# Routing tokens two chunks at a time, and moving steps of a fused attention and mixture-of-experts kernel

## What is computed

```python
x = x + tanh(g_xattn) * (softmax(q @ concat(ctx, k_new).T / 16) @ concat(ctx, v_new)) @ wo.T   # of layernorm(x)
...
probs = softmax(xf @ gate_w.T); top_p, top_i = top_k(probs, 2)
y = sum over the two experts of top_p * (silu(xf @ fc1.T) * (xf @ fc2.T)) @ proj.T
y = y + sigmoid(xf @ shared_gate_w.T) * (silu(xf @ s_fc1.T) * (xf @ s_fc2.T)) @ shared_proj.T
x = x + tanh(g_ffn) * y
```

## Time and profile before

| | |
|---|---|
| median of 3 runs (lowest, highest) | 294.89 us (294.42, 295.42) |
| the profiled execution's own time | 294.28 us |
| its span | 292.5 us |
| busy: PE, DVE, ACT, POOL | 93%, 73%, 58%, 47% of the span |
| granted clock of TensorE, mean | 0.999 |
| chain that ended last, by engine | PE 57%, DVE 23%, issue 7%, ACT 6%, DMA 3% |
| stages, by start | opening 0, chunk 0 about 17, chunk 1 about 41, chunk 2 about 65, chunk 3 about 88, shared blocks about 110, experts about 180, tail about 267 |

### The profile page before, as it was taken

The page is one execution under the profiler, slowest core; times in us unless marked ns, Lnnn a source line. Parts: engine busy times, 40 slices in busy tenths (PEclk is TensorE's granted clock), DMA queues, the critical chain, the costliest instruction groups (busy, mean ns, idle before and its releaser), DMA issues.

```text
span 292.5 us, 5859 instructions
## 1 busy us (share of the span) xinstructions
PE 272.9 (93%) x1777; PEld 245.7 (84%) x1777; DVE 213.9 (73%) x694; ACT 170.7 (58%) x401; POOL 136.1 (47%) x161
## 2 busy tenths in 40 slices
PE   3998899999899899999999999899999999999992
PEld 3887789789778677888788888899999999998882
DVE  6867776979869759768776767868778777763285
ACT  2775678687566567473335446566666667654240
POOL 2420831441784427453450000068778778776141
PEclk9999999999999999999999999999999999999999
DMA  6470244221136112544425744368888888756796
GB/s 194 190 256 2 73 149 141 72 80 50 38 91 242 74 40 85 186 144 125 150 76 182 247 140 145 131 113 134 136 141 134 136 139 137 116 69 72 291 354 217
DMA packets 25022, 40.18 MB, mean 137 GB/s; under 512 B 2976, under 2 KB 18976, under 8 KB 24992
## 3 DMA queue, kind: packets, MB, share of 16 engines
q1 hardware_dynamic: 16272, 27.43, 29.1%
q0 software_dynamic: 7152, 9.57, 19.4%
q10 hardware_dynamic: 1568, 2.80, 2.7%
HBM read 22.68 MB, written 17.11 MB: 136 GB/s over the span
## 4 chain that ended last, share of the span: by engine, by line
PE 57%; DVE 23%; issue 7%; ACT 6%; DMA 3%; POOL 1%; SPq 0%; DVEq 0%; ACTq 0%; POOLq 0%
PE bank L437 43%; PE bank L702 8%; DVE ew_lo L1097 4%; DMA xn_all<-x_dram 3%; PE bank L801 3%; PE bank L755 3%; DVE work L1453 2%; ACT ew_hi L830 2%; DVE xt_lo L1097 2%; ACT sh_hi L830 2%; DVE neg_max L1145 2%; DVE sh_lo L1097 2%; DVE ln_stats L1108 1%; DVE work L1168 1%; ACT work L862 1%
## 5 line engine op out<-in xcount | busy, mean ns | idle before, releaser
L1650 POOL DMA_INDIRECT y_d<-work,dest_of_slot x39 | 60.5, 1552 | 56.2 <-DVE dest_of_slot L1504 54.7
L437 PE MATMUL bank<-ew_hi,xt_hi 128*128 (+2 forms) x172 | 53.9, 323 | 1.4 <-DVE xt_lo L1097 0.7
L437 PE MATMUL bank<-ew_lo,xt_hi 128*128 (+2 forms) x172 | 51.7, 301 | 0.0
L437 PE MATMUL bank<-ew_hi,xt_lo 128*128 (+1 forms) x133 | 40.5, 305 | 0.0
L1610 POOL DMA_INDIRECT xs_d<-xn_all,slot_of_pair x32 | 33.3, 1042 | 10.1 <-issue 7.3
L1097 DVE TENSOR_TENSOR xt_lo<-bank,xt_hi 128x256 fp32r<-128x256 f32 (+2 forms) x90 | 35.5, 397 | 3.2 <-ACT xt_hi L830 2.0
L437 PE MATMUL bank<-xt_hi,sw_hi 128*128 128x512 f32 x88 | 34.8, 395 | 0.2 <-DVE work L1453 0.2
L437 PE MATMUL bank<-xt_lo,sw_hi 128*128 128x512 f32 x88 | 34.5, 392 | 0.0
L437 PE MATMUL bank<-xt_hi,sw_lo 128*128 128x512 f32 x88 | 34.3, 390 | 0.0
L830 ACT ACTIVATE xt_hi<-bank 128x256 fp32r<-128x256 f32 (+1 forms) x90 | 32.7, 409 | 2.4 <-PE bank L801 1.1
L437 PEld LDWEIGHTS bank<-ew_hi,xt_hi 128*128 128x128 f32 (+1 forms) x172 | 32.4, 189 | 2.0 <-DVE xt_lo L1097 0.9
(11 more groups left out here) (161 smaller groups left out, 678.8 us busy)
## 6 DMA issues: line engine op xcount, KB each, us to landing
work<-xs_d SPq DMA_DIRECT2D x39, 136.0 KB, 2.5
weight_stage<-ew_dram SPq DMA_DIRECT2D x10, 486.5 KB, 3.7
y_d<-work SPq DMA_DIRECT2D x6, 512.0 KB, 3.9
work<-ctx_t_dram SPq DMA_DIRECT2D x4, 512.0 KB, 3.3
ew_hi<-y_d SPq DMA_DIRECT2D x4, 512.0 KB, 8.1
ew_hi<-y_d ACTq DMA_DIRECT2D x4, 512.0 KB, 7.0
xn_all<-x_dram SPq DMA_DIRECT2D x3, 512.0 KB, 6.6
xs_d<-pad_row SPq DMA_DIRECT2D x9, 136.0 KB, 2.0
```

The lines of the kernel that those rows point to most:

```text
L437: last = nc.tensor.matmul(dst, a, b, start=(n == 0), stop=(n == len(pairs) - 1))
L1650: nc.gpsimd.indirect_dma_start(out=y2_d, out_offset=bass.IndirectOffsetOnAxis(ap=IX[:, n:n + 1], axis=0), in_=EY[:, n % 4, :], in_offset=None,
```

## The change

What it does, part by part:

1. **Opening.** SP loads x of chunk 1 before the context of chunk 0. ACT loads the constants before the gates. TensorE's empty products (`warm`) are 13, 0, 3 in place of 10, 4, 4. DVE does `project_lo(0, 0)` after the lo parts of the weights, `ln1_stats(2)` after `row_max(0, 2)`, and `project_lo(1, 0)` before `residual(0, 0)`.
2. **Chunks 1 and 2.** In chunk 1 `scores` alternate with `first_norm`. In chunk 2 `attend(2, 2)` and `residual(2, 2)` come after the last projection.
3. **Routing.** Two passes of 8 tiles in place of four of 4. The first (chunks 0, 1): `shifted`, `route_exp` in chunk 2, all else in chunk 3, with `slots(0)` after `aggregate(3, 0)`; `attend` doesn't wait for it. The second (chunks 2, 3) in the shared blocks, at the places of the old fourth one. POOL scatters chunk 0 in chunk 3 and the others after it.
4. **Tail.** `fc` 2 and 3, and 4 and 5, stand together; the multiply of block 5 comes before `s_lo(4)`; POOL's `combine(6)` waits for the last `s_lo`; DVE's `combine(7)` comes before `s_last`.

```diff
+GT = 2 * TPC
+N_GR = N_T // GT
...
+            load_x(1)
             sp.dma_start(CR, ctx_t[0]).then_inc(d_ct, 16)
-            load_x(1)
...
-                if j == 1 and c > 1:
-                    waits = waits + [(0, v_pos, c - 1)]
...
-            def route(c):
-                bank, o = (B[1], 0) if c == LAST else (B[7], D)
+            def route(g):
+                bank = B[4] if g == 0 else B[1]
...
-            warm(10)
+            warm(13)
             first_norm(0, 0)
-            warm(4)
             first_norm(0, 1)
-            warm(4)
+            warm(3)
...
-                if 0 < c < LAST:
+                if c == 1:
                     first_norm(c + 1, 0)
+                    scores(c, 0)
                     first_norm(c + 1, 1)
-                scores(c, 0)
-                scores(c, 1)
+                    scores(c, 1)
...
-                if c > 1:
-                    route(c - 2)
...
                 attend(c, 1)
+                if c == LAST:
+                    route(0)
...
-                attend(c, 2)
+                if c != LAST - 1:
+                    attend(c, 2)
                 values(c, 3)
                 probs_t(c, 3)
                 if c < LAST:
                     project(c + 1, 3)
+                if c == LAST - 1:
+                    attend(c, 2)
...
             fc(0, 1)
-            route(LAST - 1)
             second_norm(LAST, 0)
...
             fc(LAST, 1)
+            pj(LAST, 0)
+            fc(LAST, 2)
+            fc(LAST, 3)
+            pj(LAST, 1)
+            fc(LAST, 4)
+            fc(LAST, 5)
             for j in range(2, S_BLK):
-                if j < S_FULL:
-                    pj(LAST, j - 2)
-                fc(LAST, j)
-            for j in range(S_FULL - 2, S_BLK):
                 pj(LAST, j)
...
+            act.dma_start(C[:], consts).then_inc(d_const, 16)
             act.dma_start(G[:], gates).then_inc(tanh_g, 16)
-            act.dma_start(C[:], consts).then_inc(d_const, 16)
...
-                if c > 0:
-                    route_exp(c - 1)
+                if c == LAST - 1:
+                    route_exp(0)
...
-            ln1_stats(2)
             v_lo(0, 0)
...
             row_max(0, 2)
+            ln1_stats(2)
             v_lo(0, 1)
             probs_lo(0, 1)
+            project_lo(1, 0)
             residual(0, 0)
-            project_lo(1, 0)
...
-                if c > 1:
-                    two_best(c - 2)
+                if c == LAST:
+                    two_best(0)
                 v_lo(c, 0)
                 probs_lo(c, 0)
-                if c > 1:
-                    counts(c - 2)
+                if c == LAST:
+                    counts(0)
...
                 residual(c, 0)
-                if c > 1:
-                    slots(c - 2)
...
+                if c == LAST:
+                    slots(0)
                 v_lo(c, 2)
...
-                    shifted(c - 1)
+                if c == LAST - 1:
+                    shifted(0)
...
-            two_best(LAST - 1)
-            counts(LAST - 1)
...
-                        slots(LAST - 1)
                         logits(LAST)
-                        shifted(LAST)
+                        shifted(1)
...
             for j in range(S_BLK):
-                s_mult(LAST, j)
-                if j in (3, 5):
-                    combine((0, 4)[j // 5])
+                if j < S_FULL:
+                    s_mult(LAST, j)
+                if j == 3:
+                    combine(0)
+                if j == S_FULL - 1:
+                    s_mult(LAST, S_FULL)
+                if j == S_FULL:
+                    combine(4)
                 s_lo(LAST, j)
                 if j == 3:
                     combine(2)
+            combine(7)
             for t in range(TPC):
                 s_last(t)
-            combine(7)
...
-                if c > 1:
-                    scatter(c - 2, 0)
                 rstd2(c, 0)
+                if c == LAST:
+                    scatter(0, 0)
...
-                if 1 < c < LAST:
-                    scatter(c - 2, 1)
             rstd2(LAST, 1)
-            scatter(LAST - 2, 1)
-            for c in (LAST - 1, LAST):
+            scatter(0, 1)
+            for c in range(1, N_CH):
                 for i in range(TOP):
                     scatter(c, i)
...
             for n in (1, 3, 5, 6):
+                if n == 6:
+                    pool.wait_ge(v_hl, 6 * N_CH)
                 combine(n)
```

More of the change, by code:

```diff
@@ L743, in blocks @@
                         if order[n] == (1, 0):
-                            route(LAST)
+                            route(1)
                         if order[n] == (1, 1):
@@ L1219, in two_best, with shifted @@
-            def two_best(c):
-                dve.wait_ge(a_r, c + 1)
-                step(nc.vector.reduce_sum(RS[:, 1, 0:TPC], te(1), AX_X))
-                step(nc.vector.reciprocal(RS[:, 2, 0:TPC], RS[:, 1, 0:TPC]))
-                step(nc.vector.tensor_tensor(te(2), te(1), over_e(RS[:, 2, 0:TPC]), ALU.mult))
-                for j in range(TPC):
-                    ins = nc.vector.max(V8[:, c * TPC + j, :], te(2)[:, j, :])
+            def shifted(g):
+                t = slice(g * GT, (g + 1) * GT)
+                dve.wait_ge(v_lg, 2 * g + 2)
+                step(nc.vector.reduce_max(RS[:, 0, 0:GT], LG[:, t, 0:N_E], AX_X))
+                nc.vector.tensor_tensor(te(0), LG[:, t, 0:N_E], over_e(RS[:, 0, 0:GT]), ALU.subtract).then_inc(v_sh, 1)
@@ L1227, in two_best @@
+            def two_best(g):
+                dve.wait_ge(a_r, g + 1)
+                step(nc.vector.reduce_sum(RS[:, 1, 0:GT], te(1), AX_X))
+                step(nc.vector.reciprocal(RS[:, 2, 0:GT], RS[:, 1, 0:GT]))
+                step(nc.vector.tensor_tensor(te(2), te(1), over_e(RS[:, 2, 0:GT]), ALU.mult))
+                for j in range(GT):
+                    ins = nc.vector.max(V8[:, g * GT + j, :], te(2)[:, j, :])
                 step(ins)
-                for j in range(TPC):
-                    ins = nc.vector.max_index(I8[:, c * TPC + j, :], V8[:, c * TPC + j, :], te(2)[:, j, :])
+                for j in range(GT):
+                    ins = nc.vector.max_index(I8[:, g * GT + j, :], V8[:, g * GT + j, :], te(2)[:, j, :])
@@ L1230, in two_best, with counts @@
                 step(ins)
                 best = RS[:, 3, :].rearrange("p (i t) -> p i t", i=TOP)
-                step(nc.vector.tensor_copy(best, I8[:, c * TPC:(c + 1) * TPC, 0:TOP].rearrange("p t i -> p i t")))
-            def counts(c):
+                step(nc.vector.tensor_copy(best, I8[:, g * GT:(g + 1) * GT, 0:TOP].rearrange("p t i -> p i t")))
+            def counts(g):
                 best = RS[:, 3, :].rearrange("p (i t) -> p i t", i=TOP)
-                if c == 0:
+                if g == 0:
@@ L1238, in counts @@
                     dve.wait_ge(d_rc, 16)
                 for i in range(TOP):
-                    step(nc.vector.tensor_tensor(et(3 + i), constants(R_IOTA, TPC),
-                                                 best[:, i, :].unsqueeze(1).broadcast_to([P, N_E, TPC]), ALU.is_equal))
-                step(nc.vector.tensor_tensor(SX[:, :, 1:TPC + 1], et(3), et(4), ALU.add))
-                nc.vector.tensor_tensor_scan(out=CUM.rearrange("p e j -> p (e j)"), data0=RC[:, R_SCAN:R_SCAN + N_E * (TPC + 1)],
+                    step(nc.vector.tensor_tensor(et(3 + i), constants(R_IOTA, GT),
+                                                 best[:, i, :].unsqueeze(1).broadcast_to([P, N_E, GT]), ALU.is_equal))
@@ L1244, in counts, with slots @@
+                step(nc.vector.tensor_tensor(SX[:, :, 1:GT + 1], et(3), et(4), ALU.add))
+                nc.vector.tensor_tensor_scan(out=CUM.rearrange("p e j -> p (e j)"), data0=RC[:, R_SCAN:R_SCAN + N_E * (GT + 1)],
                                              data1=SX.rearrange("p e j -> p (e j)"), initial=0.0, op0=ALU.mult, op1=ALU.add)\
                     .then_inc(v_oh, 1)
-            def slots(c):
-                dve.wait_ge(p_r, c + 1)
-                at = B[7][:, D:D + NB].rearrange("p (e t) -> p e t", e=N_E)
-                if c == LAST:
-                    nc.vector.tensor_copy(KEEP, B[1][:, 0:N_E * (TPC + 1)]).then_inc(v_keep, 1)
+            def slots(g):
+                dve.wait_ge(p_r, g + 1)
+                at = B[4][:, 0:NB].rearrange("p (e t) -> p e t", e=N_E)
+                if g == N_GR - 1:
+                    nc.vector.tensor_copy(KEEP, B[1][:, 0:N_E * (GT + 1)]).then_inc(v_keep, 1)
@@ L1339, in _ @@
             ln1_stats(1)
-            project_lo(0, 0)
             weight_lo(2)
             weight_lo(3)
+            project_lo(0, 0)
             project_lo(0, 1)
@@ L1528, in _ @@
                     if (s, j) == (0, 3):
-                        two_best(LAST)
+                        two_best(1)
                     if (s, j) == (0, 4):
-                        counts(LAST)
+                        counts(1)
                     if (s, j) == (0, 5):
```

(2 more changed lines are left out.)

85 lines of the change are left out of this document (45 added, 40 removed).

## The result

The changed kernel took 297.26 us (median of 6 runs, 296.88 to 297.61) against 294.77 us for the kernel before (6 runs, 294.31 to 295.84): a ratio of 1.0067, 95% interval 1.0040 to 1.0095. The forecast was 290.5 us (range 288.2 to 292.7), so both its sign and its range were missed.

What follows compares the result with a forecast made beforehand. TensorE, busy 93% of the span, was taken as the bound, its late starts mostly waiting for DVE's lo parts. Terms 0.8 + 0.3 + 1.4 + 0.7 + 0.8 + 0.8 - 1.2 + 0.8 = 4.4 us gave 290.5 us, range 288.2 to 292.7.

Steps and rivals of the forecast that it cites:

- The opening, +0.8: Chunk 0: reordered loads and DVE steps shorten TensorE's waits despite a context 1.4 us late; 0.8 us faster.
- chunk 1, +0.3: Chunk 1: a `scores` in between fills part of TensorE's 0.57 us wait for `first_apply(2)`; 0.3 us faster.
- Chunk 2, +1.4 for `slots(0)`: Chunk 2: without `slots(0)` on DVE, the lo parts TensorE awaits until 77.43 come in time; 1.4 us faster.
- What would show it: The prediction's list of profile signs, such as no routing steps on DVE in chunk 2 and TensorE's L1468 wait over a microsecond.
- Chunk 2, +0.7 for `attend(2, 2)`: End of chunk 2: the moved `attend(2, 2)` fills TensorE's wait before `scores(3, 0)` at 87.88; 0.7 us faster.
- Chunk 3 and into the shared blocks, +0.8 and +0.8: Chunk 3: 2.1 us of waits won against longer pass, net 0.8; `two_best`, `counts`, `route(2)` leaving attention's end, another 0.8.
- The second pass, -1.2: Shared blocks: the 8-tile pass is 1.0 to 1.2 us longer and TensorE has no slack there; 1.2 us slower.
- Scatters, 0: POOL's scatters after the last `slots` end before SP's tile loads at 176.19, with 7 us cover; no cost.
- Rival E: Before the experts: the scatters become their gate, making the kernel slower, 297.1 us; chance 0.04.
- The tail, +0.8: Kernel's end: last `s_lo` no longer held by POOL's add, so the last store's issue ends 0.8 us earlier.
- rival B: Tail: POOL's `combine(6)` starts first and holds DVE's `combine(7)` 1.27 us; tail gives 0.2, total 291.1 us; chance 0.16.
- D: Whole kernel: no measurable change, as late context, blocks and lower ends eat the gains; 294.0 us; chance 0.06.

Runs made afterwards that it cites:

- routing_only: The kernel before with the paired routing (part 3) alone: 293.96 us, ratio 0.9975.
- opening_only: The kernel before with the opening's edits (part 1) alone: 294.33 us, ratio 0.9998.
- late_pool_op: The kernel before with one small GpSimd instruction, which nothing waits for, held until TensorE's last product: 298.4 us, ratio 1.0127.
- no_tail: The changed kernel with the tail of the kernel before: 294.50 us, ratio 0.9988.
- no_hold: The changed kernel without the wait of GpSimd's `combine(6)` for the last `s_lo`: 297.45 us, ratio 1.0080.
- routing_c2: routing_only with `attend(2, 2)` and `residual(2, 2)` also moved behind chunk 3's projection: 296.64 us, ratio 1.0039.
- routing_again: A repetition of routing_only in another series and on another chip: 294.30 us, ratio 0.9959.
- mended: The changed kernel without the moved `attend(2, 2)` and `residual(2, 2)`, and with `combine(6)` on DVE behind the last sums: 293.65 us, ratio 0.9953.
- pair_dve_six: The kernel before with paired routing, regrouped tail and `combine(6)` on DVE, without the opening and chunk 1 edits or moved attend: 295.56 us, ratio 1.0024.
- pair_regroup: As pair_dve_six, but `combine(6)` stays on GpSimd, not held: 295.75 us, ratio 1.0019.
- dve_six: As no_hold, but `combine(6)` moves from GpSimd to DVE behind the last sums, its store behind SyncE's last two: 295.59 us, ratio 1.0037.

## Why the prediction was wrong

Step by step, with the forecast's terms:

- **The opening, +0.8, and chunk 1, +0.3.** 0.05 in the profile by 55.33, and 0.9998 for the opening by itself. Executions differ by more than this there (the table's first row runs from -0.76 to +0.92).
- **Chunk 2, +1.4 for `slots(0)`.** Right: 1.5 in the changed kernel and in routing_only. As listed under "What would show it", DVE has no routing step there and the wait at 77.43 shrinks to 0.39.
- **Chunk 2, +0.7 for `attend(2, 2)`.** Wrong in its sign: -0.8 in all (the gap gave 0.2, `neg_max` took 1.0). I priced the products that fill TensorE's gap at 87.88, and not DVE's `residual(2, 2)` that moves with them. For the routing's steps the prediction asked what is queued behind them on DVE; for this move it did not. The idle time that it left was free; the place that it took stood before `neg_max`.
- **Chunk 3 and into the shared blocks, +0.8 and +0.8.** In routing_only they net 0.05 between 91.17 and 119.96. The two waits at 97.89 and 99.32 gave 0.95 in place of 2.1 (the later start of the first `attend`, 1.05, was sized rightly at 1.0 to 1.2). `slots(0)` does hide in DVE's idle time, as the timeline of the changed kernel shows:

```profile
100.51 0.19 DVE L1269 TENSOR_TENSOR work<-work,bank 128x64 f32<-128x64 f32 x1
...
101.90 0.20 DVE L1272 SCALAR_TENSOR_TENSOR slot_of_pair<-work 128x16 uint32<-128x16 f32 x1
102.13 0.17 DVE L1274 COPY work<-work 128x8 f32<-128x8 f32 x1
102.75 1.02 DVE L1107 TENSOR_TENSOR ew_lo<-bank,ew_hi 128x512 fp32r<-128x512 f32 x2 [0.44 <-ACT ew_hi L837]
```

  The idle time before this `ew_lo` is 0.44, where the earlier trace rows has 1.74. But `route(0)` now stands among TensorE's products here, 0.4 us, and of the 1.1 won before 115 the blocks take 0.5 back by 117.7.
- **The second pass, -1.2.** Right for the cost that it names: -1.53 to -0.33 in routing_only, -1.2. The wait for L1468 grew to the 0.67 of this row, its start 1.4 later than in before:

```profile
142.04 0.35 PE L708 MATMUL bank<-sw_hi,sh_hi 128*128 128x256 f32 x1 [0.67 <-DVE work L1480]
```

  I had expected over a microsecond in the bracket. In routing_only another 0.4 goes by 171, in the changed kernel none.
- **Scatters, 0.** Right: nothing new stands before the expert tiles, and from 138.74 to 267.61 the shift changes by 0.12. Rival E didn't occur; that its 297.1 us stands next to the measured 297.26 is chance.
- **The tail, +0.8.** This is the step that failed. The products are 1.1 earlier against the start of the tail, as worked out, and DVE's `combine(7)` (286.99) started before POOL's addition (287.16), so rival B didn't occur either: POOL was the one held, 1.69 in place of 1.27. But I took the end from the issue of the last store, read as if the kernel ended with it. The end is the later of two: the last landing, and GpSimd's end. The prediction priced the wait of `combine(6)` at nothing, since DVE's path was what counted, and never asked what ends behind that addition. It also left out that the store of `combine(6)`'s rows, issued at 286.39 in before, now leaves at 288.87, among the last ones, which land later for it. By terms, each against the 1.3 us by which the tail begins late: the last issue ends 1.1 earlier (forecast 0.8), the landing behind it takes 0.8 longer, and GpSimd's end lies 1.5 further behind the landing. The net of the tail was -1.2 in place of +0.8. One thing more weakens this term: the wait of 1.25 that it was to remove is the largest of the six profiles with the tail of before and no new instruction or wait in it (0.22 in opening_only, 0.45 to 0.81 in the others), as it depends on which DVE instruction the landing of POOL's rows happens to meet.

In the profile of the changed kernel the shifts sum so: 0.05 + 1.53 - 0.82 + 0.15 - 1.10 - 1.21 + 0.12 + 1.10 for the products, -0.2 us in all, and then -2.3 at the end. The forecast had 4.4. Of the distance some 2.0 is the tail, 1.5 the moved attend, 1.5 chunk 3, 1.1 the opening and chunk 1, and 1.1 the step that stays open, which no term of the forecast names. (A slip without weight: half way between rivals B and D is 292.55, not 292.7.)

## What to carry to other kernels

A wait that is put on an engine to keep it out of another's way also moves the last instruction of that engine, and this can be what the kernel's end waits for: read what every engine does behind its last row, and end GpSimd's part early (here 6.1 us before the end of the span). When a step is moved to fill a gap, its partners on the other engines move too, so name what each of them leaves (idle time is worth nothing) and what it lands ahead of. Time won before a fixed queue of work, as by the routing in chunk 2, is worth only what the next stage with no slack doesn't take back.

## What the hardware showed that I had not expected

**GpSimd's end.** Its DRAIN record ends 5.86 to 5.89 us after its last vector instruction in each of the profiles, be that instruction 1.84 us or 0.20 us long; DVE's, ACT's and TensorE's take 0.15 to 1.45 us in all in before. The Trainium skill (Runtime: NRT & Kernel Launch, "The ~15µs preamble/postamble breakdown") has the closing barrier wait for all engines, at about 1.5 us; it gives no time for GpSimd. Here the span ends 0.23 us behind GpSimd's DRAIN where this comes last, so the 5.9 us come ahead of that, and no run here shows the barrier's own time. What fills the 5.9 us no run here shows; all kernels here issue indirect DMAs from GpSimd, so none shows whether it needs them.

**TensorE's clock falls in chunk 3, in some executions.** These views of late_pool_op and, last, of before have stretches of time and, as the number behind the busy times, the granted clock:

```profile
97.00:100.00 3.00, 1.59 (x9) 1.01 (x8) 2.79 (x9) 0.64 (x3) 1.44 (x3) 1.00 0.02 5
100.50:104.00 3.50, 3.50 (x17) 3.26 (x15) 0.90 (x4) 0.95 (x3) 2.79 (x6) 0.53 0.46 174
```

```profile
97.00:100.00 3.00, 1.58 (x9) 1.05 (x8) 2.65 (x9) 0.64 (x3) 1.58 (x3) 1.00 0.03 13
```

After a stretch in which TensorE was busy for 1.59 of 3 us, the clock is at its lower level, 1.2 in place of 2.4 GHz, for about 3.5 us. But the profile of before has the same stretch, 1.58 of 3 us, and no fall behind it, so the stretch alone doesn't bring it. Five of the sixteen profiles have one such fall, two at 100.5 to 100.7 (late_pool_op, opening_only), which cost 1.1 to 1.5 us, and three at 94.0 to 94.6 (no_tail, no_hold, routing_c2), which cost 0.6. Of the 111 executions of the kernel before in the four series 34 have a mean granted clock of 0.992 or less, and their medians are 1.0 to 1.9 us above those of the rest. The kernels with the paired routing and without the moved attend (routing_only, routing_again, mended, pair_dve_six, pair_regroup) have none in 60. So a part of the routing's 0.25 to 0.4% may come from there. It isn't the whole: against the executions of before above 0.992 alone (medians 294.52 and 295.11), routing_only is still 0.6 us and routing_again 0.8 us faster. With the move, 6 of 12 have it again in routing_c2 and 4 of 12 in dve_six, but 1 of 12 in no_tail.

Two things limit this count. The mean takes in the end of the span too, where TensorE has nothing left to do and the clock falls: the changed kernel's 0.993 is nothing but 1.2 GHz from 290.9 to 295.0. And late_pool_op, which differs from before only behind the last addition, lies at 0.981 to 0.987 in five of six executions, further down than its end alone takes it (by 0.007), where before has 4 of 22 at 0.992 or less in the same series. So something else than the order of work in chunk 3 also decides how often the clock falls. Why one stretch of waits brings it and another not was not tested.

**A step that stays open.** In the profiles of six kernels, all with the paired routing, ScalarE begins `s_hi(0, 2)` 0.4 to 1.7 us later than TensorE's records allow. The changed kernel and mended:

```profile
119.55 1.01 ACT L837 ACTIVATE ew_hi<-weight_stage 128x973 fp32r<-128x973 f32 x1
123.56 0.63 ACT L837 ACTIVATE sh_hi<-work 128x512 fp32r<-128x512 f32 x1 [3.01 <-PE bank L708]
```

```profile
119.45 1.01 ACT L834 ACTIVATE ew_hi<-weight_stage 128x973 fp32r<-128x973 f32 x1
122.37 0.63 ACT L834 ACTIVATE sh_hi<-work 128x512 fp32r<-128x512 f32 x1 [1.92 <-PE bank L705]
```

The release comes from `pj(0, 0)`; in the changed kernel its last recorded product starts at 122.1, and the signal is counted at 123.48, 1.4 us behind; in before the two are 0.3 apart. `pj(0, 0)` also waits for DVE's `logits(3)`, ahead of its last three products, but this had ended at 121.02 and isn't the cause. The Trainium skill (Perfetto Trace Analysis, "Tensor Engine Instruction (MATMUL, LD_WEIGHTS)") says that the ends of TensorE's records are estimated, so they can't say where the 1.1 us went. no_tail, with the same routing and move, has no such delay, nor have routing_only, routing_again and mended; pair_dve_six and pair_regroup have it without the move. What does divide the ten profiles with the paired routing is the series: all five of the second and third have the delay, and the changed kernel's own, and none of the four of the first and fourth. So it may belong to the chip or the moment as much as to an edit, and one profile a kernel can't tell these apart. It is 1.1 us of the changed kernel's profile, and neither its cause nor how often it occurs was settled. It may be why pair_dve_six (1.0024) and mended (0.9953), which are of different series and differ by opening and chunk 1 alone, lie so far apart; this is argued and not shown.
